# Gathers ahead of the late pieces, row work on GpSimd, and no products of a cleared tile

## The reference

```python
x = x + attention(layernorm(x))
x = x + ffn(layernorm(x))

# attention: 16 heads of 8 values
q, k, v = h @ Wq, h @ Wk, h @ Wv
latent  = (k + v) @ W_down_kv              # 32 wide
k_rec, v_rec = latent @ W_up_k, latent @ W_up_v
scores = clip(q_head @ k_head.T / sqrt(128)) * exp(-1e-4 * |i - j|)
out    = softmax(scores) @ v_head @ Wo

# ffn: rows divided by input_scale and rounded to float8_e4m3, the same for
# the 128x128 kernel; y = (rows @ kernel) * scales, to bf16, + bias
```

## Time and profile before

| what | value |
|---|---|
| median of 3 runs | 566.92 us (564.33 to 570.27) |
| the profiled execution | 570.72 us, span 568.9 us |
| TensorE busy | 500.9 us, 88% |
| ScalarE busy | 487.1 us, 86% |
| VectorE busy | 309.9 us, 54% |
| GpSimd busy | 185.4 us, 33% |
| 512 exponentials (L681) | 479.7 us |
| ScalarE's wait before them for VectorE's corrections (L1100) | 42.9 us in 28 waits |
| mean granted TensorE clock | 0.953 |
| transfers | 73.77 MB, mean 130 GB/s |
| first and last exponential | start 18.35 us, end 546.9 us |

### The profile page before, as it was taken

One profiled execution on the slowest core, in us unless ns is written; L12 is line 12 of the kernel. 1 busy time (PEld: TensorE's weight loads), 2 busy tenths in 40 slices (PEclk: granted clock), 3 DMA queues, 4 the chain that ended last, 5 costly groups with the idle time before them and its releaser, 6 DMA issues.

```text
span 568.9 us, 9341 instructions
## 1 busy us (share of the span) xinstructions
PE 500.9 (88%) x3456; PEld 115.4 (20%) x3456; DVE 309.9 (54%) x743; ACT 487.1 (86%) x528; POOL 185.4 (33%) x170
## 2 busy tenths in 40 slices
PE   8866971999899999999799999998999999999971
PEld 3310210222112121222112221222111211122220
DVE  4523330355865466566665566557556555456646
ACT  1654980799899999998899999998999999999951
POOL 0787600488433002969052003968000001000100
PEclk9996995899999999999899999999899999999985
DMA  6248978046599710075797600086796400000000
GB/s 190 87 170 228 367 199 156 6 159 216 174 255 202 170 45 6 6 279 191 203 246 146 147 10 5 5 315 222 169 248 151 109 6 6 24 20 2 1 18 22
DMA packets 48705, 73.77 MB, mean 130 GB/s; under 512 B 6096, under 2 KB 26512, under 8 KB 48528
## 3 DMA queue, kind: packets, MB, share of 16 engines
q1 hardware_dynamic: 47840, 72.85, 46.1%
q10 hardware_dynamic: 816, 0.28, 0.2%
HBM read 35.40 MB, written 35.65 MB: 125 GB/s over the span
## 4 chain that ended last, share of the span: by engine, by line
PE 43%; ACT 26%; DVE 7%; issue 7%; DMA 6%; POOL 5%; SPq 4%; ACTq 0%; POOLq 0%; DVEq 0%
ACT probs L681 26%; PE ps L876 22%; PE ps L860 12%; DMA qp_dram<-parts 3%; DVE ps L1100 2%; DMA o_raw<-pv_out 2%; PE ps L742 1%; PE ps L779 1%; PE ps L774 1%; POOL sq L566 1%; POOL parts L568 1%; PE ps L751 1%; SPq L387 1%; SPq L395 1%; DMA kp_dram<-parts 1%
## 5 line engine op out<-in xcount | busy, mean ns | idle before, releaser
L681 ACT ACTIVATE probs<-ps 128x1024 f32<-128x1024 f32 x512 | 479.7, 1067 | 48.8 <-DVE ps L1100 42.9
L876 PE MATMUL ps<-probs,V 128*9 128x512 f32 x2048 | 272.2, 603 | 19.1 <-DVE pv_out L1108 16.7
L1100 DVE TENSOR_TENSOR ps<-ps,consts 128x256 f32<-128x256 f32 (+1 forms) x256 | 143.8, 565 | 171.5 <-PE ps L860 163.8
L860 PE MATMUL ps<-Qs,Ks 64*128 64x512 bf16 x992 | 183.4, 390 | 27.4 <-ACT probs L681 11.4
L860 PEld LDWEIGHTS ps<-Qs,Ks 64*128 64x128 bf16 x992 | 43.9, 93 | 303.2 <-ACT probs L681 278.4
L602 POOL TENSOR_TENSOR xs<-xs,magic 128x512 f32<-128x512 f32 x7 | 8.9, 1278 | 244.6 <-DVE magic L1160 244.6
L876 PEld LDWEIGHTS ps<-probs,V 128*9 128x9 f32 x2048 | 31.3, 88 | 96.0 <-issue 74.5
L554 POOL TENSOR_TENSOR sq<-kT,decay 128x256 f32<-128x256 f32 (+2 forms) x13 | 16.6, 1277 | 80.6 <-DVE kT L1209 49.3
L1108 DVE COPY pv_out<-ps 105x512 f32<-105x512 f32 x31 | 21.4, 691 | 38.0 <-PE ps L876 21.7
L568 POOL TENSOR_TENSOR parts<-sq,parts 128x1024 bf16<-128x1024 f32 (+1 forms) x17 | 31.1, 1832 | 1.4
L566 POOL TENSOR_TENSOR sq<-sq,parts 128x1024 f32<-128x1024 f32 (+1 forms) x17 | 30.5, 1794 | 1.4
(11 more groups left out here) (138 smaller groups left out, 273.6 us busy)
## 6 DMA issues: line engine op xcount, KB each, us to landing
Qs<-qp_dram SPq DMA_DIRECT2D x26, 512.0 KB, 9.8
qp_dram<-parts SPq DMA_DIRECT2D x16, 768.0 KB, 6.2
Ks<-kp_dram SPq DMA_DIRECT2D x26, 384.0 KB, 6.3
kp_dram<-parts SPq DMA_DIRECT2D x12, 384.0 KB, 3.8
kp_dram<-parts SPq DMA_DIRECT2D x6, 768.0 KB, 4.4
qp_dram<-parts SPq DMA_DIRECT2D x8, 512.0 KB, 7.4
Qs<-qp_dram SPq DMA_DIRECT2D x12, 256.0 KB, 4.8
X<-L_attn_x SPq DMA_DIRECT2D x10, 256.0 KB, 3.0
```

Of the source, the lines that this page charges most:

```text
L681: nc.scalar.activation(probs[:, quad % RING, 2 * jp:2 * jp + 2, :].rearrange("p j n -> p (j n)"), ps_all[:, bank * CH:(bank + 2) * CH], AC ...
L860: last = nc.tensor.matmul(bank, Ks[half, g, jp, key_cols(v, kc)], Qs[half, g, jp, qh, v, :], start=True, stop=True)
L876: last = nc.tensor.matmul(pv[32 * j:32 * j + VW, :], V[:, unit // 2 * NB + kc, HG * j + g, :], probs[:, quad % RING, j, :], start=i == 0, ...
L1100: nc.vector.tensor_tensor(own, own, factors, ALU.mult).then_inc(fixed, 1)
```

## The change

Six things are changed.

1. SyncE, batch 0: `store_qk(0)`, the late pieces' stores, their loads and group 0's `stage` leave the code ahead of the loop. They are issued in it by `late_pieces(g)`: after `gather(0)` the late keys' stores and `store_qk(0)`, after `gather(1)` the late queries' stores, group 0's loads and the late loads of groups 1 to 3. The early keys of a next batch are stored after the gather of group 2, not of group 3.
2. GpSimd computes the inverse deviation of the rows (`rows_istd`, 14 steps) and adds bias and residual (`result`); VectorE's `inverse_std_step` calls in `tail`, `add_bias` and `result` go. VectorE waits for `istd_ready` at the normalising step and for `res_ready` ahead of the next y.
3. `tail` of the rows handled in odd units of the first three batches normalises at quad 23 in place of 21, divides at 24, makes the grid at 26 and quantises at 29 and 30; their xqT and y jobs stand at 34 and 36 in place of 30 or 34 (`TAIL_ROWS`, `TAIL_PRODUCTS`). The flag's two jobs move from quads 4 and 6 to 14 and 18 of unit 6.
4. GpSimd splits the first queries from `Q0` (`split_queries_of_first_group`), without `decayed_queries`. The late keys of batch 0 are made ahead of `normalise(1)`.
5. The first query projection and `first_queries(PLUS)` stand ahead of the first key projection and `first_keys`.
6. `keep_busy` and the clearing of its tile go.

```diff
@@ -119,15 +119,18 @@
+TAIL_ROWS = [28 if not is_shared(_u) else 34 if _u % 2 else 30 for _u in range(UNITS)]
+TAIL_PRODUCTS = [30 if not is_shared(_u) else 36 if _u % 2 else 34 for _u in range(UNITS)]
 for _u in range(1, UNITS):
     JOBS += [(_u * UNIT_QUADS + _q, _k, _u - 1) for _q, _k in (
-        (10, "sp"), (12, "proj"), (30 if is_shared(_u) else 28, "xqT"), (34 if is_shared(_u) else 30, "y"))]
+        (10, "sp"), (12, "proj"), (TAIL_ROWS[_u], "xqT"), (TAIL_PRODUCTS[_u], "y"))]
 for _b in range(B - 1):
     JOBS += [(_b * STREAM + _q, _k, 2 * (_b + 1) + _h) for _q, _k, _h in (
         (14, "T", 0), (18, "T", 1), (22 if _b else 26, "k", 0), (26 if _b else 28, "k", 1),
         (28 if _b else 30, "q", 0), (36, "q", 1), (38, "v", 0), (46, "v", 1))]
     JOBS += [(_b * STREAM + 60, "n", _b + 1)]
-JOBS += [(3 * STREAM + 4, "flags", 0), (3 * STREAM + 6, "flag", 0)]
+JOBS += [(3 * STREAM + 14, "flags", 0), (3 * STREAM + 18, "flag", 0)]
 JOBS += [((UNITS - 1) * UNIT_QUADS + _q, "turn", _g) for _g, _q in enumerate((14, 18, 26))]
...
@@ -446,19 +451,22 @@
                 load_queries(0, g, slice(0, 1), stage_in[g])
-            store_qk(0)
             load_x1(0)
             load_x1(1)
-            store_keys(0, "late keys", slice(0, KL), 0)
-            store_queries(0, "late queries", 1)
-            sp.wait_ge(parts_out[0], 16 * STORED * 3)
-            sp.wait_ge(parts_out[1], 16 * STORED * 2)
-            for g in range(F32_GROUPS, G):
-                load_keys(0, g, slice(0, KL), stage_late[g])
-                load_queries(0, g, slice(1, 2), stage_late[g])
-            sp.wait_ge(qk_done, 2 * NB * F32_GROUPS)
-            for g in range(F32_GROUPS):
-                stage(0, g)
+            def late_pieces(g):
+                if g == 0:
+                    store_keys(0, "late keys", slice(0, KL), 0)
+                    store_qk(0)
+                elif g == 1:
+                    store_queries(0, "late queries", 1)
+                    for first in range(F32_GROUPS):
+                        stage(0, first)
+                    for later in range(F32_GROUPS, G):
+                        load_keys(0, later, slice(0, KL), stage_late[later])
+                        load_queries(0, later, slice(1, 2), stage_late[later])
             for unit in range(UNITS):
@@ -468,8 +476,11 @@
                         gather(group)
+                    if unit == 0:
+                        late_pieces(g)
+                    if qh == 0 and g == 2 and b < B - 1:
+                        store_keys(b + 1, "early keys", early, 0)
                     if qh == 0 and g == 3 and b < B - 1:
-                        store_keys(b + 1, "early keys", early, 0)
                         store_queries(b + 1, "early queries", 0)
...
@@ -564,6 +575,16 @@
                 chain(nc.gpsimd.tensor_tensor(r, r, to[0], ALU.subtract))
+                chain(nc.gpsimd.tensor_copy(to[1], r))
+                chain(nc.gpsimd.tensor_tensor(to[2], r, to[1], ALU.subtract))
+                pool.sem_inc(parts_ready, 1)
+            def split_queries_of_first_group():
+                r, q = rest, Q0.rearrange("p v n -> p (v n)")
+                to = [parts[:, 1, k, :] for k in range(PARTS)]
+                chain(nc.gpsimd.tensor_copy(to[0], q))
+                chain(nc.gpsimd.tensor_tensor(r, q, to[0], ALU.subtract))
                 chain(nc.gpsimd.tensor_copy(to[1], r))
@@ -584,10 +605,13 @@
                 split(1, S, 0)
-            def late_parts(b):
-                stored_before(b, 0, 2 if b == 0 else 1)
+            def late_keys(b):
+                stored_before(b, 0, 1)
                 decayed_keys(PLUS, slice(2 * P, KP), 0)
                 split(0, KL, 0)
+            def late_queries(b):
                 pool.wait_ge(q_sb, 2 * b + 2)
@@ -601,6 +625,20 @@
                 nc.gpsimd.tensor_tensor(xs[:, :], xs[:, :], magic[:, :], ALU.subtract).then_inc(rounded, 1)
+            def rows_istd(unit):
+                pool.wait_ge(moments_ready, unit + 1)
+                inverse_std(mv2, rs2)
+                pool.sem_inc(istd_ready, 1)
+            def result(unit):
+                own = X1[:, unit % 2, :]
+                y3 = yb[:, :].rearrange("p (t d) -> p t d", d=D)
+                pool.wait_ge(y_ready, unit + 1)
+                chain(nc.gpsimd.tensor_tensor(y3, y3, bias_s[:, :].rearrange("p (o d) -> p o d", o=1)
+                                              .broadcast_to([P, 4, D]), ALU.add))
+                nc.gpsimd.tensor_tensor(own, own, yb[:, :], ALU.add).then_inc(res_ready, 1)
             pool.wait_ge(decay_in, 16)
@@ -608,31 +646,42 @@
             split(0, CH, 0)
-            pool.wait_ge(q_sb, 1)
-            decayed_queries(0)
-            split(1, S, 0)
+            pool.wait_ge(q0_ready, 2)
+            split_queries_of_first_group()
             pool.wait_ge(k_sb, 2)
             decayed_keys(MINUS, slice(CH, S), 0)
             split(0, CH, CH)
+            late_keys(0)
             normalise(1)
-            late_parts(0)
+            late_queries(0)
             squares(0)
             for b in range(B):
                 if 0 < b < B - 1:
                     normalise(b + 1)
                 if b > 0:
+                    result(2 * b - 2)
+                    rows_istd(2 * b - 1)
                     to_grid(2 * b - 1)
                 if b < B - 1:
                     early_parts(b + 1)
-                    late_parts(b + 1)
+                    if b > 0:
+                        result(2 * b - 1)
+                    late_keys(b + 1)
+                    late_queries(b + 1)
                     squares(b + 1)
+                else:
+                    result(2 * b - 1)
+                rows_istd(2 * b)
                 to_grid(2 * b)
+            result(UNITS - 2)
             pool.wait_ge(flag_ready, 1)
             general = pool.value_load(flag[0:1, 0:1], min_val=0, max_val=1)
             with pool.If(general > 0):
                 for unit in range(UNITS, 2 * UNITS):
+                    rows_istd(unit)
                     to_grid(unit)
+                    result(unit)
             with pool.Else():
@@ -711,23 +760,14 @@
         def _(pe):
-            def keep_busy(times):
-                for _ in range(times):
-                    nc.tensor.matmul(ps[:, 0, :], xn2[:, 0:P], xn2[:, :], start=True, stop=True)
-            pe.wait_ge(tiles_clear, 1)
-            keep_busy(9)
             pe.wait_ge(w_in, 32)
             pe.wait_ge(fold_in, 48)
             nc.tensor.matmul(ps[0:DL, 7, 0:D], wd_s[:, :], wkT_s[:, :], start=True, stop=False)
             nc.tensor.matmul(ps[0:DL, 7, 0:D], wd_s[:, :], wvT_s[:, :], start=False, stop=True).then_inc(fold_pe, 1)
-            keep_busy(2)
             pe.wait_ge(fold_act, 1)
             nc.tensor.matmul(ps[:, 6, 0:D], wdown_T[:, :], wuk_s[:, :], start=True, stop=True)
             nc.tensor.matmul(ps[:, 6, D:2 * D], wdown_T[:, :], wuv_s[:, :], start=True, stop=True).then_inc(fold_pe, 1)
-            keep_busy(7)
             def transpose_x(n, bank):
@@ -834,10 +874,11 @@
             transpose_x(0, ps[:, 4, :])
+            pe.wait_ge(wq_in, 16)
+            pe.wait_ge(xnT_ready, 1)
+            project_q(0, ps[:, 6, :])
             pe.wait_ge(fold_act, 3)
             project_k(0, ps[:, 5, :])
-            pe.wait_ge(wq_in, 16)
-            project_q(0, ps[:, 6, :])
             transpose_x(1, ps[:, 7, :])
...
@@ -1050,11 +1090,11 @@
             dve.wait_ge(const_in, 16)
+            dve.wait_ge(q_ps, 1)
+            first_queries(PLUS, ps[:, 6, :])
             dve.wait_ge(k_ps, 1)
             first_keys(0, PLUS, slice(0, 2 * P), ps[:, 5, 0:2 * P]).then_inc(km0_ready, 1)
             first_keys(0, MINUS, slice(2 * P, CH), ps[:, 5, 2 * P:CH]).then_inc(km0_ready, 1)
-            dve.wait_ge(q_ps, 1)
-            first_queries(PLUS, ps[:, 6, :])
             first_queries(MINUS, ps[:, 6, :])
@@ -1140,9 +1180,10 @@
                     step(nc.vector.bn_aggr(mv2[:, t, :], stats2[:, t, :]))
+                settle()
             def normalise_rows(unit, tiles):
-                settle()
+                dve.wait_ge(istd_ready, unit + 1)
                 for t in tiles:
@@ -1169,16 +1210,6 @@
                                                    op1=ALU.add).then_inc(xq_ready, 1)
-            def add_bias():
-                y3 = yb[:, :].rearrange("p (t d) -> p t d", d=D)
-                step(nc.vector.tensor_tensor(y3, y3, bias_s[:, :].rearrange("p (o d) -> p o d", o=1)
-                                             .broadcast_to([P, 4, D]), ALU.add))
-            def result(unit):
-                settle()
-                own = X1[:, unit % 2, :]
-                nc.vector.tensor_tensor(own, own, yb[:, :], ALU.add).then_inc(res_ready, 1)
             def divide_rows_by_sums(g, bank, tiles, count):
@@ -1238,6 +1269,7 @@
                     dve.wait_ge(y_ps, i + 1)
+                    dve.wait_ge(res_ready, i)
```

(41 more changed lines are left out.)

## The result

The changed kernel took 545.35 us (542.74 to 547.04, 4 runs) against 567.75 for the kernel before in the same comparison: ratio 0.9605, 95% interval 0.9537 to 0.9673, or 22.4 us less where 29.6 were forecast. The profiled execution of the first comparison took 547.04 us, span 545.2, the slowest of its four.

The account below looks back on a forecast made before the run. ScalarE's exponentials were taken to set the pace, so only its waits could be gained. Terms -17.9 + 1.0 - 1.2 - 12.5 + 1.0 = -29.6 us took the median 566.9 to 537.3, range 530 to 548.

Parts of the forecast that it names:

- the queue rival: SyncE's queue: late loads land after unit 1 begins, or a gather behind them stops a copy; 542 to 548, chance 0.12.
- a unit past the first longer than 62: Sign set beforehand: any unit after the first taking more than 62 us would show the prediction wrong.
- The other sign: At the start: the float32 group ending after 45 us would show the prediction wrong.
- (a): Quads 24 to 32, first pass: gathers go ahead of late pieces, so the copy no longer waits; -17.9 us.
- (b): Start of unit 1: TensorE waits for group 0's late loads; +1.0 us, bounds 0 and +5.
- (c): The start: GpSimd drops the 2.37 us product, first keys come 1.2 later; -1.2 us net, -3 at full clock, +2 worst.
- (d): TensorE's clock without cleared-tile products: slower early quads covered by the 6.93 us wait for loads; 0, else 1 to 3 us.
- (e): GpSimd takes VectorE's small steps and adds; waits in units 1, 3, 5 go: -12.5 us, collisions about +1.0.
- The rival of VectorE waiting for GpSimd: Shared port lock: instructions moved to GpSimd block VectorE, giving back 8 to 23 us; 545 to 560, chance 0.12.

Follow-up runs that it names:

- the second profile: The changed kernel itself measured and profiled again, nothing altered, six runs: 543.64 us, ratio 0.9571 to the kernel before.
- the store back: Changed kernel with the next batch's early keys stored after gather(3) again, not ahead of it: 544.29 us, ratio 0.9601 to the kernel before.
- the queue alone: Kernel before with only SyncE's new order (late pieces behind gather(0) and gather(1), early keys stored ahead of gather(3)): 542.94 us, ratio 0.9561.
- the share alone: Kernel before with only GpSimd's inverse deviation, bias and residual and the later quads in odd units: 559.17 us, ratio 0.9853.
- the queue with the store back: Kernel before with only SyncE's new order, but early keys of the next batch stored behind gather(3) as before: 549.17 us, ratio 0.9656.
- the last experiment: Changed kernel with cleared-tile products back, early keys stored behind gather(3), and VectorE's reciprocals at quad 8 instead of 7: 540.67 us, ratio 0.9538.
- the start alone: Kernel before with only the start's new order (first query projection and queries ahead of keys), cleared-tile products kept: 565.11 us, ratio 0.9960.

## Why the prediction was right, and where it was off

The measured 22.4 us are 7.2 short of the sum, and 545.35 lies in the range of the queue rival too (542 to 548): the profiled execution shows what that rival names, a late gather and the clock lost once more, though at the reciprocals and not at a copy. By its own sign, a unit past the first longer than 62, the prediction was wrong in that execution, with 66.4; the second profile has none above 61.1. The other sign, a float32 group that ends after 45, did not come.

**(a), right in cause and size.** 33.5 to 16.0, and the wait for the gather is gone.

**(b), the wrong place.** TensorE did not wait for group 0's loads at the start of unit 1. What was late next was a step I called ahead of need "by a group": gather(3). I held it against the copy that reuses its buffer and overlooked that the reciprocals at quad 7 of the next unit need the last gather of the unit. Its price is 5.3 us in the first profile of the changed kernel (66.4 against 61.1 with the store back), with the fall of the clock, and nothing in the second (61.1). Over several runs putting the store back gained nothing that could be measured.

**(c) and (d), the step that failed.** "Their cover is the 6.93 us wait for the loads: 0". The wait is the end of a chain that starts at the first key projection: projection, copy, GpSimd's splits, stores, loads. What slows the head of a chain isn't covered by the wait at its end. With the new order two projections stand at that head, and the products decide whether they take 2.0 or 3.8 us from start to end. I had put -1.2 against -3 at the full clock into (c), and taken the lower clock as given on the side of the change while reading the side of before from one execution in which the clock had risen only at 13.8 us. In other kernels with products and the old start (the queue alone, the share alone, the queue with the store back) it rose between 4.9 and 5.8 and group 1's first exponential came at 45.3, 44.1 and 44.2, not at 46.93; the changed kernels without products had it at 46.2, 46.4, 46.0 and 46.5. So against those the start became 0.7 to 2.4 us later rather than 1.2 earlier, and with the products it was 4.5 better than it became. Some 1.9 of the 4.5 are the stores' late landing, which no term of the sum had.

**(e), right in cause, too large, and wrong in whose it was.** Units 3 and 5 gained 4.4 and 4.1 us where 4.7 each was forecast, and unit 1 gained 1.9 in the second profile, where the stop is absent: 10.4 us together where 12.5 were put in, and GpSimd was never late for VectorE's normalising step. But the queue's part takes most of the same waits away. Alone, the share gives 8.4 us, the queue 24.9 by its ratio, the start 2.3, the products 0.3: 35.9 together, 22.4 to 24.4 measured. With the queue and the start in place, adding the share is worth 0.6 us by the medians (541.27 to 540.66) and 2.7 by the profiled spans.

**The lock.** The rival of VectorE waiting for GpSimd came true at one place, the spread at quad 7 (quad 8 in the last experiment): 1.56 to 1.61 us in place of 0.69 in one unit of each of four profiles, 1.07 to 1.13 in one or two units of three. The rule cited from the Trainium skill ("SBUF — State Buffer", "SBUF: two separate sides"), that a VectorE instruction with two SBUF inputs and a GpSimd instruction exclude each other for the whole of the one that holds the ports, agrees with the spread, which has two such inputs, in both directions: 1.56 us where GpSimd began first, and GpSimd's 1.51 in place of 1.16 where the spread did. The two small steps of the earlier trace rows and 1.82 us after it are not of that form: they read one SBUF tile (`rs<-mv`, `rs<-rs`), and yet end with GpSimd's instruction. So the prediction's reading, "the ends at 269.17 and 270.99 agree", holds for the waiting, not for the form that it names. The corrections kept their 0.70 us.

**The reference.** The terms were read from an execution of 570.72 us and taken from the median of 566.9. Its late rise of the clock (13.8 us) and its full waits in units 1, 3 and 5 (193.3 us together; 191.9 and 190.9 in two other profiles with the same queue) are partly its own. From profile to profile the change gives 23.7 us with the bad stop and 27.8 without it (span 541.1); from median to median 22.4 and 24.5. So with the stop absent the sum of 29.6 is close for the execution it was read from, and some 3 us of the gap to the medians come from that choice.

## What to carry to other kernels

When a step is moved past another in an in-order queue, list everyone who waits for the passed step, not only the one that reuses its buffer. A wait hides only work that does not feed it: before calling a slower head of the program covered by a later wait, follow that wait back to its source. And when two parts of a change are both credited with the same stall, try one alone: here the place of one store, 5.4 us, did much of what the moved arithmetic was meant to do, 8.4 alone. When the same transfer lands later in one kernel than in another, look in the trace for what else was transferred at that time, instruction queues included.

## What the runs showed of the hardware

The clock rises at a different time in executions of nearly the same start: with the products at 4.6 to 5.8 us in eight profiles and at 13.8 in one, without them at 15.4 to 17.9 in five. In eight of the nine profiles with products the rise is thus 9.6 us or more earlier than in those without. In the kernel with the start alone it fell again at 11.7 for 3.4 us, after TensorE had stood still for 0.73, 0.93 and 0.77 us; in three other kernels with products and the new start TensorE had pauses of 0.7 to 1.2 us at the same places and the clock stayed.

The landing of the same three stores took 7.0 to 8.9 us after the first issue. In all fourteen profiles 98% of their packets have ended 6.4 to 6.5 us after it. The last packet ends at 6.5 to 6.6 us in five profiles, where a 16 KB transfer of the instruction queue falls ahead of the stores' packets, and at 8.0 to 8.1 in four, where it falls toward their end. Without the products this transfer came at 35.2 to 37.4 us, with them at 26.9 to 32.0. Whose instructions it brings was not tested.
